# A fused cross-attention decoder on one core: another order of steps inside the software-pipelined batch loop, other PSUM banks, more waits ahead of TensorE's first matmul

## The reference

```python
def layer(x, ctx):                       # x [256, 256], ctx [77, 256]
    x = x + attn(rms(x) @ wq0, ctx @ wk0, ctx @ wv0) @ wo0
    x = x + attn(ln(x) @ mq, ln(x) @ mk, ln(x) @ mv, causal=True) @ mp
    x = x + attn(ln(x) @ cq, ctx @ ck, ctx @ cv) @ cp
    return x + relu(ln(x) @ f1) @ f2     # biases left out here
```

## Time and profile before

| | us |
|---|---|
| median of three runs (5142.68 to 5169.89) | 5162.13 |
| the profiled execution | 5167.24 |
| its span | 5165.4 |
| of it the 61 turns of the loop | 4560.0 |
| the head and the tail | 393.7, 211.7 |

### The profile page before, as it was taken

The page is one execution under the profiler, slowest core; times in us unless marked ns, Lnnn a source line. Parts: engine busy times, 40 slices in busy tenths (PEclk is TensorE's granted clock), DMA queues, the critical chain, the costliest instruction groups (busy, mean ns, idle before and its releaser), DMA issues. The chain is left out here.

```text
span 5165.4 us, 143863 instructions
## 1 busy us (share of the span) xinstructions
PE 4860.0 (94%) x47160; PEld 3984.5 (77%) x47160; DVE 3085.7 (60%) x8003; ACT 3954.5 (77%) x16437; POOL 539.3 (10%) x845
## 2 busy tenths in 40 slices
...
DMA packets 220219, 183.58 MB, mean 36 GB/s; under 512 B 111312, under 2 KB 203920, under 8 KB 219856
## 3 DMA queue, kind: packets, MB, share of 16 engines
...
## 5 line engine op out<-in xcount | busy, mean ns | idle before, releaser
L924 ACT ACTIVATE ps<-ps,negmax 128x77 f32<-128x77 f32 (+2 forms) x6144 | 2074.3, 383 | 192.8 <-DVE negmax L1174 190.8
L924 ACT ACTIVATION_READ_ACCUMULATOR ps<-ps,negmax 128x1 f32 x6144 | 1551.1, 260 | 0.0
L1174 DVE TENSOR_REDUCE negmax<-ps 128x4 f32<-128x308 f32 (+2 forms) x1792 | 939.9, 562 | 215.7 <-PE ps L1484 124.8
L876 POOL TENSOR_TENSOR small<-small 128x1 f32<-128x1 f32 (+1 forms) x448 | 264.0, 589 | 4569.8 <-DVE small L1151 2618.1
L1018 ACT ACTIVATE probs<-ps 128x512 f32<-128x512 f32 x768 | 403.0, 602 | 240.3 <-PE ps L1565 238.1
L1484 PE MATMUL ps<-k0bd,q0T 128*128 128x154 f32 x2048 | 373.1, 305 | 18.0 <-ACT ps L924 10.2
L1169 DVE TENSOR_TENSOR aTl<-ps,aTh 128x256 fp32r<-128x256 f32 x256 | 102.3, 420 | 454.8 <-ACT aTh L904 454.8
L904 ACT COPY probs<-ps 77x512 f32<-77x512 f32 x512 | 279.0, 582 | 98.2 <-PE ps L1527 97.9
L1484 PEld LDWEIGHTS ps<-k0bd,q0T 128*128 128x128 f32 x2048 | 289.6, 191 | 72.6 <-ACT ps L924 27.3
L1250 DVE RECIPROCAL over<-sums 128x4 f32<-128x4 f32 x512 | 88.2, 172 | 417.5 <-ACT ps L924 417.5
L1380 PE MATMUL ps<-hi_wo,coTh 128*128 128x256 f32 x1024 | 328.5, 321 | 0.0
...
## 6 DMA issues: line engine op xcount, KB each, us to landing
keys_of<-kring SPq DMA_DIRECT2D x128, 154.0 KB, 1.9
k0bd<-keys_of SPq DMA_DIRECT2D x128, 154.0 KB, 3.2
...
```

The costliest lines, as they stand in the source:

```text
L876: nc.gpsimd.tensor_tensor(rstd[:, stage, ts], veps[:, stage, ts], minus_half[:, ts], ALU.pow).then_inc(rstd_ready[stage], 1)
L924: ins = nc.scalar.activation(scores, scores, ACT.Exp, bias=negmax[w][:, t, h:h + 1], accum_out=sums[w][:, t, h:h + 1])
L1174: nc.vector.tensor_reduce(dst, bank(s)[:, 0:heads * width].rearrange("p (h k) -> p h k", h=heads), AX_X, ALU.max, negate=True).then_inc(ma ...
```

## The change

The steps, their matmuls and shapes, and the number of turns stay. The orders of PE, ACT and DVE in the loop, the batch parts of the head, and the tail are other ones, the banks too; the loop is cut at another step, so that ACT branches back in front of `pv.1.0`'s copy and no longer behind it; two steps fewer stand in the head and two more in the tail. PE waits 190 times for the constants, where it waited 34 times.

```diff
 LOOP_ORDER_TEXT = """
-ln.2 rms+ skA.1:6015 qs0.1.3-:4 pv0.0-:3 pv0.1-:2 pv.1.1:7 turn.0+:0 tr0.0.2-:5 proj.1.0:7 proj.1.1:4 tr0.1.2-:7
+pv.1.0:4 skA.1:7613 qs0.0.2-:5 qs0.1.2-:4 rms+ pv0.0-:2 pv.1.1:3 stat.2.0 tr0.1.2-:1 proj.1.0:7 stat.2.1 proj.1.1:4
...
 DVE_ORDER_TEXT = """
-turn.3.1 qsA/1 qsA/0 qsA/2 h.3/0 qs0.1.1/0 h.3/1 h.2/0 h.0/0 h.2/1 ln.1 h.0/1 h.1/0 qs0.1.0/0 qs0.0.3/0 h.1/1
+rms pv.1.0 qs0.1.2/0 norm.0 qs0.0.2/0 qs0.1.2/1 pv.1.1 qs0.0.2/1 proj.1.0 proj.1.1 stat.2.0 stat.2.1 norm.2.0
...
-            for _ in range(34):
+            for _ in range(190):
                 pe.wait_ge(consts_made, 9)
```

More of the change, by code:

```diff
@@ L55 @@
-tr0.0.1+:4 tr0.0.0+:3 qs0.0.3+:6 h.1:5 mt.1-:3 qs0.1.0+:0 skB-:2134 f2.0:5 skA.0-:7432 ln.1- tr0.1.0+:0 norm.0+
-stat.3.1 qs0.1.2+:6 tr0.1.1+:1 norm.3.0 f2.1:7 qs0.0.2+:4 pv.1.0-:2 norm.3.1
+pv.1.0:4 skA.1:7613 qs0.0.2-:5 qs0.1.2-:4 rms+ pv0.0-:2 pv.1.1:3 stat.2.0 tr0.1.2-:1 proj.1.0:7 stat.2.1 proj.1.1:4
+pv0.1-:7 tr0.0.2-:6 tr0.0.3-:3 norm.2.0 turn.0+:4 turn.2.0:0 tr0.1.3-:6 turn.2.1:5 pv0.2-:1 stat.1.0- q1.2:3
+norm.1.0- pv0.3-:4 qs2.1:0321 stat.1.1- qs2.0:7564 wo.0-:0 norm.0+ norm.1.1- norm.2.1 wo.1-:2 q0.1+:4 q0.0+:0
@@ L57 @@
+turn.1.0-:2 turn.1.1-:6 qs0.0.1+:4 q0.3+:3 mt.2:1 k1-:5 sk2.0:1673 qs0.0.0+:0 sk2.1:2456 q1.1-:3 pv.2.0:4 norm.3.0
+qsB.1-:2731 pv.2.1:6 v1-:5 proj.2.0:6 qsB.0-:4710 proj.2.1:5 q0.2+:2 turn.3.0:4 qsA-:6350 turn.3.1:2 qs0.1.1+:7 ln.2
+tr0.0.1+:1 h.1:4 h.3:2 qs0.0.3+:3 h.2:7 tr0.1.1+:5 ln.1- h.0:6 tr0.0.0+:5 qs0.1.0+:0 mt.1-:2 stat.3.0 qs0.1.3+:1
+stat.3.1 skB-:5742 f2.0:6 skA.0-:5470 f2.1:2 norm.3.1 tr0.1.0+:6
 """
 ACT_ORDER_TEXT = """
-skA.1/3 skA.1/2 skA.1/0 skA.1/1 qs0.1.3 pv.1.1 turn.0 tr0.0.2 pv0.0 tr0.1.2 tr0.1.3 q0.0 turn.2.0 turn.2.1 pv0.1
@@ L63 @@
[L63 to L67, removed]
+pv.1.0 skA.1/0 skA.1/2 skA.1/1 skA.1/3 qs0.1.2 pv.1.1 qs0.0.2 pv0.0 tr0.0.2 tr0.1.2 tr0.0.3 turn.2.0 turn.2.1 turn.0
@@ L68 @@
+tr0.1.3 pv0.2 pv0.1 q1.2 pv0.3 qs2.1/0 qs2.1/2 qs2.0/1 qs2.1/1 qs2.0/3 qs2.0/0 qs2.1/3 qs2.0/2 q0.1 ln.2 turn.1.0
+q0.0 turn.1.1 qs0.0.1 mt.2 q0.3 k1 sk2.0/1 sk2.0/3 sk2.0/2 sk2.0/0 sk2.1/0 sk2.1/1 q1.1 pv.2.0 sk2.1/2 sk2.1/3
+qs0.0.0 pv.2.1 qsB.1/3 qsB.1/1 qsB.1/0 v1 qsB.1/2 qsB.0/0 qsB.0/3 q0.2 qsB.0/1 turn.3.0 qsB.0/2 turn.3.1 qsA/1
+qs0.1.1 qsA/0 qsA/2 qsA/3 tr0.1.1 ln.1 tr0.0.1 tr0.0.0 mt.1 qs0.1.0 skB/1 skB/2 skB/0 skB/3 qs0.0.3 skA.0/0 skA.0/1
+skA.0/2 skA.0/3 qs0.1.3 tr0.1.0
 """
 DVE_ORDER_TEXT = """
-rms qs0.1.3/0 norm.0 qs0.1.3/1 pv.1.1 turn.0 proj.1.0 stat.2.0 proj.1.1 stat.2.1 norm.2.0 norm.2.1 turn.2.0 turn.2.1
@@ new lines @@
+norm.2.1 turn.2.0 turn.2.1 turn.0 pv0.0 pv0.2 pv0.1 qs2.1/0 pv0.3 qs2.1/1 qs2.1/2 qs2.0/1 qs2.1/3 qs2.0/3 qs2.0/2
+qs2.0/0 wo.0 stat.1.0 wo.1 norm.1.0 stat.1.1 norm.1.1 ln.2 turn.1.0 qs0.0.1/0 turn.1.1 qs0.0.1/1 qs0.0.0/0 pv.2.0
+qsB.1/0 qsB.1/3 qsB.1/1 pv.2.1 qs0.0.0/1 qsB.1/2 proj.2.0 stat.3.0 qsB.0/0 qsB.0/3 proj.2.1 norm.3.0 qsB.0/1
+stat.3.1 qsB.0/2 norm.3.1 qsA/1 turn.3.0 turn.3.1 qs0.1.1/0 qsA/0 qsA/2 h.1/0 qs0.1.1/1 h.1/1 qsA/3 h.3/0 h.2/0
+h.3/1 ln.1 h.2/1 h.0/0 h.0/1 qs0.1.0/0 qs0.1.3/0 qs0.0.3/0 qs0.1.0/1 qs0.0.3/1 f2.0 f2.1 qs0.1.3/1
@@ L172 @@
+qs0.0.2@0/0 qs0.1.3@0/1 qs0.1.2@0/0 qs0.0.3@0/1 pv0.1@0 qs0.0.2@0/1 qs0.1.2@0/1 pv0.0@0 w.13@0 pv0.3@0 pv0.2@0
+qs0.0.0@1/0 qs0.1.0@1/0 wo.0@0 qs0.1.1@1/0 stat.1.0@0 qs0.0.0@1/1 norm.1.0@0 wo.1@0 stat.1.1@0 norm.1.1@0
+qs0.1.1@1/1 turn.1.0@0 turn.1.1@0 qs0.0.1@1/0 qs0.1.0@1/1 qs0.0.1@1/1 w.12@0 qsB.0@0/0 qsB.0@0/1 qsB.0@0/3 qsB.1@0/2
+qsB.1@0/0 qsB.1@0/1 qsB.0@0/2 qsB.1@0/3 qsA@0/2 qsA@0/3 qsA@0/1 qsA@0/0 ln.1@0 qs0.0.3@1/0 qs0.0.3@1/1 qs0.1.3@1/0
+qs0.1.3@1/1
 """
 TAIL_ORDER_TEXT = """
-rms@2 ln.1@2 skA.1@0:3065 stat.2.0@0 qs0.1.3@1:1 pv0.0@1:7 tr0.1.2@1:5 pv.1.1@0:0 pv0.1@1:7 ln.2@2 proj.1.0@0:3
@@ L175 @@
[L175 to L189, removed]
@@ L190 @@
[L190 removed]
+ln.2@1 qs0.1.2@1:0 qs0.0.2@1:2 pv.1.0@0:3 skA.1@0:4671 rms@2 pv0.1@1:5 tr0.1.3@1:1 stat.2.0@0 tr0.0.3@1:2 stat.2.1@0
+pv.1.1@0:0 pv0.0@1:4 proj.1.0@0:3 tr0.0.2@1:0 proj.1.1@0:6 pv0.3@1:3 tr0.1.2@1:1 turn.2.0@0:2 stat.1.0@1 turn.0@2:1
+turn.2.1@0:7 pv0.2@1:0 q1.2@0:2 ln.1@1 qs2.1@0:6521 q0.1@2:7 wo.0@1:0 norm.1.0@1 qs2.0@0:1427 norm.2.0@0 wo.1@1:5
+stat.1.1@1 qs0.1.1@2:1 qs0.0.1@2:2 q0.0@2:6 q0.2@2:0 norm.2.1@0 q0.3@2:5 mt.2@0:4 turn.1.0@1:2 norm.1.1@1
@@ new lines @@
+turn.1.1@1:7 qs0.0.0@2:6 sk2.1@0:3041 q1.1@1:5 sk2.0@0:7213 k1@1:0 tr0.1.1@2:6 tr0.0.1@2:1 pv.2.1@0:5 pv.2.0@0:4
+qsB.1@1:2307 proj.2.0@0:5 proj.2.1@0:6 qsA@1:1504 qs0.1.0@2:7 qsB.0@1:2361 turn.3.1@0:7 turn.3.0@0:4 qs0.0.3@2:2
+h.2@0:4 h.0@0:6 v1@1:1 h.3@0:4 tr0.0.0@2:7 tr0.1.0@2:1 mt.1@1:5 h.1@0:6 stat.3.0@0 norm.3.0@0 stat.3.1@0 norm.3.1@0
+stat.2.0@1 stat.2.1@1 skA.0@1:5730 qs0.0.2@2:1 skB@1:4260 stat.1.0@2 f2.1@0:3 pv.1.0@1:6 skA.1@1:1427 qs0.1.2@2:0
+f2.0@0:5 qs0.1.3@2:2 pv.1.1@1:1 pv0.1@2:7 proj.1.1@1:5 stat.1.1@2 proj.1.0@1:0 pv0.0@2:5 tr0.1.2@2:4 norm.2.0@1
@@ new lines @@
+tr0.0.2@2:6 tr0.0.3@2:2 tr0.1.3@2:3 pv0.2@2:4 turn.2.0@1:1 turn.2.1@1:0 pv0.3@2:2 q1.2@1:1 qs2.1@1:2135 norm.2.1@1
+qs2.0@1:7640 wo.0@2:1 wo.1@2:0 turn.1.1@2:4 mt.2@1:7 turn.1.0@2:2 sk2.1@1:6750 norm.1.0@2 sk2.0@1:2134 ln.2@0 k1@2:6
+q1.1@2:5 pv.2.1@1:3 pv.2.0@1:1 qsB.1@2:0762 proj.2.0@1:5 qsB.0@2:4365 norm.1.1@2 stat.3.0@1 proj.2.1@1:1 v1@2:0
+turn.3.0@1:2 qsA@2:1674 turn.3.1@1:3 norm.0@2 h.0@1:2 h.1@1:5 h.2@1:3 h.3@1:4 mt.1@2:7 skB@2:1750 skA.0@2:2346
+f2.0@1:0 stat.3.1@1 norm.3.0@1 pv.1.0@2:4 skA.1@2:2710 norm.3.1@1 stat.2.0@2 f2.1@1:3 pv.1.1@2:7 stat.2.1@2
@@ L191 @@
+proj.1.0@2:5 proj.1.1@2:1 turn.2.0@2:5 turn.2.1@2:0 norm.2.0@2 q1.2@2:1 norm.2.1@2 qs2.1@2:2603 qs2.0@2:1475
+mt.2@2:2 ln.2@2 norm.3.0@2 sk2.0@2:3756 sk2.1@2:4123 pv.2.0@2:4 pv.2.1@2:2 proj.2.0@2:6 proj.2.1@2:0 stat.3.0@2
+stat.3.1@2 turn.3.0@2:3 turn.3.1@2:5 h.2@2:0 h.1@2:6 h.0@2:2 h.3@2:3 f2.0@2:4 f2.1@2:7 norm.3.1@2 ln.1@2
 """
 TAIL_ACT_ORDER_TEXT = """
-skA.1@0/1 skA.1@0/3 skA.1@0/0 skA.1@0/2 pv0.0@1 qs0.1.3@1 pv.1.1@0 tr0.0.3@1 tr0.1.2@1 tr0.1.3@1 turn.0@2 tr0.0.2@1
-pv0.1@1 turn.2.0@0 turn.2.1@0 pv0.3@1 pv0.2@1 q1.2@0 q0.1@2 qs2.0@0/2 qs2.0@0/3 qs2.0@0/0 qs2.0@0/1 qs2.1@0/3
@@ L200 @@
-skA.1@1/1 qs0.0.2@2 pv.1.1@1 qs0.1.2@2 pv0.0@2 tr0.0.2@2 tr0.1.2@2 tr0.0.3@2 tr0.1.3@2 turn.2.0@1 turn.2.1@1 pv0.2@2
-pv0.1@2 pv0.3@2 q1.2@1 qs2.1@1/0 qs2.1@1/3 qs2.1@1/2 qs2.1@1/1 qs2.0@1/1 qs2.0@1/3 qs2.0@1/0 qs2.0@1/2 turn.1.0@2
-ln.2@1 turn.1.1@2 mt.2@1 k1@2 sk2.0@1/2 sk2.0@1/3 sk2.0@1/1 q1.1@2 sk2.1@1/2 sk2.1@1/0 sk2.1@1/3 sk2.1@1/1 sk2.0@1/0
-qsB.1@2/1 qsB.1@2/3 pv.2.1@1 qsB.1@2/0 pv.2.0@1 qsB.0@2/2 qsB.1@2/2 qsB.0@2/1 qsB.0@2/0 qsB.0@2/3 turn.3.0@1 qsA@2/0
-turn.3.1@1 qsA@2/2 qsA@2/1 qsA@2/3 ln.1@2 v1@2 mt.1@2 skB@2/0 skB@2/2 skB@2/1 skA.0@2/2 skB@2/3 skA.0@2/1 skA.0@2/0
@@ new lines @@
+qs2.1@0/0 qs2.0@0/0 qs2.0@0/2 qs2.0@0/1 qs2.0@0/3 q0.0@2 ln.2@0 qs0.0.1@2 qs0.1.1@2 mt.2@0 q0.2@2 turn.1.0@1
+turn.1.1@1 q0.3@2 qs0.0.0@2 sk2.1@0/3 sk2.1@0/0 sk2.1@0/2 sk2.1@0/1 q1.1@1 sk2.0@0/2 sk2.0@0/0 sk2.0@0/1 sk2.0@0/3
+k1@1 pv.2.1@0 pv.2.0@0 tr0.1.1@2 tr0.0.1@2 qsB.1@1/2 qsB.1@1/0 qsB.1@1/3 qsB.1@1/1 qsA@1/0 qs0.1.0@2 qsA@1/3
+turn.3.1@0 qsB.0@1/0 turn.3.0@0 qsB.0@1/2 qsB.0@1/3 qsB.0@1/1 qsA@1/1 qsA@1/2 v1@1 ln.1@1 qs0.0.3@2 tr0.0.0@2 mt.1@1
+tr0.1.0@2 skA.0@1/3 skA.0@1/2 qs0.0.2@2 skA.0@1/0 skB@1/1 skB@1/3 skA.0@1/1 skB@1/2 skB@1/0 pv.1.0@1 skA.1@1/0
```

98 lines of the change are left out of this document (44 added, 54 removed).

## The result

The changed kernel takes 5092.86 us (median of four runs, 5089.65 to 5094.59), the kernel before 5158.72 (four runs); the ratio is 0.9874, with a 95% interval of 0.9846 to 0.9902. The forecast was 5075, from 5030 to 5165.

The account below looks back on a forecast made before the run. PE, busy 94% of the span, was taken as the bound, through full-clock turn length and number of dips. From 5167.2: -43 (turns), -56 (dips), +6 (start) = 5074, forecast as 5075 us; range 5030 to 5165.

Parts of the forecast that it names:

- the gain from the dips: Loop: 5 dips (PE clock at 0.50 for 3.41 us) instead of 45, each costing 1.39 us; -56 us.
- the gain from the turn's length: Loop at full clock: each turn 0.7 us shorter, -43 us in 61 turns; bounds -67 to +18.
- `qs2.0`: PE's wait for its fourth bank: `pv0.3`'s low part ends earlier with one maximum ahead, not two; -0.39 us a turn.
- the loop's head to `proj.1.0`: ACT's branch moved, exponentials start as PE ends, but fewer and shorter steps cover them; nearly cancels, +0.1 us a turn.
- `proj.1` to `pv0.3`: From `proj.1` to `q1.2`: the norm chain starts 0.45 later and is 0.25 shorter; +0.2 us a turn.
- `wo.0` to `mt.2`: At `mt.2`: PE's wait of 0.22 for `ln.2` ends in `q0.0` and `q0.3`, now ahead; -0.2 us a turn.
- held back for waits and overheads: PE's turn: allowance for six more register instructions and overheads the walk forgets; +0.4 us a turn.
- Rival 1: Loop: the turn shortens, but the dips stay; 5130 us, still faster; chance 0.12.
- Rival 3: Loop: every turn has a dip, 61 for 45, if full-clock turns last 73.6 or more; 5195 us; chance 0.10.
- Rival 4: Loop: the turn grows 0.7 us, as `sk2.1`'s bank and `proj.1.0` add 0.5 each; 5166 to 5190 us; chance 0.06.
- The start: Before the loop: 156 more waits make `hi_wk` start 6 us later; +6 us, bounds 3 and 8.3.
- The tail: Head and tail: same steps in sum, long waits of the last batch remain; 0, plus or minus 8 us.

Follow-up runs that it names:

- run 12: Changed kernel with 34 waits at the start and ACT's exponentials of `skA.1` in the order 3, 0, 1, 2 instead of 0, 2, 1, 3; 5068.9 us, 0.9830 of before.
- run 2: Kernel before with DVE's order alone changed: `pv0.3`'s low part ahead of the second maximum of `qs2.1`; 5105.8 us, 0.9910 of before.
- run 10: Kernel before with its loop cut one step earlier and `pv0.3`'s low part ahead of the second maximum of `qs2.1`; 5090.6 us, 0.9856 of before.
- run 3: Changed kernel with two maxima of `qs2.1` ahead of `pv0.3`'s low part again in DVE's order; 5151.9 us, 1.0002 of before.
- run 1: Kernel before with eight discarded matmuls ahead of the wait for the fourth bank of `qs2.0`; 5113.4 us, 0.9928 of before.
- run 5: Changed kernel with four discarded matmuls added in `f2.0`, where PE waits for nothing, for a longer turn; 5125.5 us, 0.9901 of before.
- run 6: Kernel before with four discarded matmuls added in `f2.0`, for a longer turn; 5168.0 us, 0.9988 of before.
- run 9: Kernel before with its loop cut one step earlier, so ACT branches ahead of `pv.1.0`'s copy; 5122.3 us, 0.9915 of before.
- run 8: Changed kernel with `pv0.3`'s low part ahead of both maxima of `qs2.1` in DVE's order; 5193.9 us, 1.0034 of before.

## Why the prediction was right, point by point

The direction, the range and the gain from the dips held; the gain from the turn's length was two thirds of what was forecast, 28 us for 43. The sum was 18 too low by the median. Its base was the profiled execution, 5 above the median of its three runs, and "5075 stands well for both" left that out. From profile to profile it is 16 too low (5089.65 for 5074): 15 by the turns, 5 by the tail and 1 by the start, less 5 by the dips. To compare piece by piece I took the distance of each step's start to the next in the full-clock turns of both traces, less the shortest that a step of its kind has in either. The sums of these by stretch give the turn's -0.44:

| stretch of PE's order | predicted | measured |
|---|---|---|
| `qs2.0` | -0.39 | -0.34 |
| the loop's head to `proj.1.0` | +0.1 | +0.51 |
| `proj.1` to `pv0.3` | +0.2 | +0.17 |
| `wo.0` to `mt.2` | -0.2 | -0.02 |
| `k1` to `sk2.1` | -0.2 | -0.16 |
| from there to `h` | -0.6 | -0.53 |
| the rest | 0 | -0.07 |
| held back for waits and overheads | +0.4 | in the rows above |

- **The step that was mis-sized is the loop's head**: "The two nearly cancel: +0.1", measured +0.51. The exponentials do start as PE ends `skA.1`, 0.03 behind it where it was 0.87. But I had counted on `pv.1.1` starting as they end. It starts 0.52 behind them, 0.39 more than before, because the last exponential's wait is the first of five in PE's queue (run 12). So the way from `skA.1` to `pv.1.1` is 0.04 longer, where it should have been some 0.35 shorter. The prediction spoke of such instructions as a cost per instruction, up to 0.64; the runs showed that what costs is where they stand behind the one that comes true last. The other 0.47 is the single transpose between `pv.1.1` and `proj.1.0`, which the prediction named: these stand 2.45 apart in both kernels, with 0.49 less work of PE between them now, hence its wait of 0.31 for `aTl`. The reserve of 0.4 made up for most of this in the sum, which is luck.
- **`qs2.0`** had the right size, but whether it counts depends on the order behind it, which the prediction did not see: in the old order it gives nothing to the turn (runs 2 and 10), in the new one all of itself (run 3). That `q0.0` makes the difference is argued, not shown.
- **`mt.2`**: the wait of 0.22 is gone from the list of waits, but the stretch from `wo.0` is as long in sum; a little went into each of its steps.
- **The dips**: 43 to none, 61 us for the 56 predicted. That the weak place is `qs2.0` and that a dip repeats through the turn's length are both shown (runs 1, 3, 5, 6). But of the two reasons given for the gain, the shorter wait alone is enough: run 2 has no dips with the old turn of 73.73, and run 5 none at 73.80. The shorter turn alone is not: run 9, at 73.46, kept 22. Rival 1 (the dips stay) fell. The rule of the Trainium skill ("TensorE: Matmul & The Clock Gate", HAM oscillation), on which that rival drew, has the clock fall behind idle stretches longer than any here; run 1 speaks against it as the only way: eight matmuls in a wait of 1.2 us took all dips away.
- **Rival 3** (every turn has a dip) did not come, though run 8 shows that an order of this kind can reach 52 in some 60 turns, in rows of up to 17, and is slower than before (1.0034). **Rival 4**'s mechanism, `proj.1.0` waiting, is there with 0.31, offset elsewhere.
- **The start**: +6 predicted, `hi_wk` 6.2 later, the loop 7.0 later. 8.40 us for 78 pairs of waits is 0.108 each, as estimated. **The tail** grew by 4.8, inside the 8 allowed; why was not tried. The old order's tail takes 211 to 216 us in the profiles, the new one's 216 to 220, so the order seems to account for most of it.
